# Moving one of the seven products of V, and the first half of P, within an attention block's instruction order

## The reference

```
h    = group_norm(x) * w + b                       # 512 x 1024
q, k, v = split(qkv_w @ h + qkv_b)                 # three times 512 x 1024
attn = softmax(q^T k / sqrt(512))                  # 1024 x 1024
o    = attn @ v^T                                  # 1024 x 512
out  = x + out_w @ o^T + out_b
```

## Time and profile before

| | |
|---|---|
| median of 3 runs | 1997.63 us (1994.39 to 1999.02) |
| the profiled execution | 1995.93 us, its span 1994.1 us |
| TensorE matmul busy | 1977.3 us (99% of the span) |
| VectorE busy | 1644.5 us (82%) |
| ScalarE busy | 1121.0 us (56%) |
| GpSimd busy | 448.8 us (23%) |
| TensorE's granted clock | 0.9 or more of full speed in each of the 40 slices |
| chain that ended last | PE 9%, DVE 4%, ACT 2%, DMA 2%, issue 1% of the span |

### The profile page before, as it was taken

One profiled execution on the slowest core, in us unless ns is written; L12 is line 12 of the kernel. 1 busy time (PEld: TensorE's weight loads), 2 busy tenths in 40 slices (PEclk: granted clock), 3 DMA queues, 4 the chain that ended last, 5 costly groups with the idle time before them and its releaser, 6 DMA issues. The chain is left out here.

```text
span 1994.1 us, 26069 instructions
## 1 busy us (share of the span) xinstructions
PE 1977.3 (99%) x9895; PEld 1679.2 (84%) x9895; DVE 1644.5 (82%) x2010; ACT 1121.0 (56%) x1431; POOL 448.8 (23%) x306
## 2 busy tenths in 40 slices
PE   9999999999999999999999999999999999999999
PEld 7888888888888888888888888887888888878788
DVE  8896987969879698796978879697796987969866
ACT  6564645646465564645656467464565646556461
POOL 1122040231412213131230401314022131221311
PEclk9999999999999999999999999999999999999999
DMA  6305143060431504324042330614306043150411
GB/s 176 128 7 138 49 75 118 6 159 28 75 118 22 170 2 75 118 54 139 6 86 101 70 123 6 146 41 75 118 11 165 17 75 118 20 172 2 75 33 54
DMA packets 102637, 157.89 MB, mean 79 GB/s; under 512 B 49377, under 2 KB 51265, under 8 KB 102513
## 3 DMA queue, kind: packets, MB, share of 16 engines
q0 software_dynamic: 31264, 73.15, 17.5%
q1 hardware_dynamic: 71248, 83.08, 12.9%
HBM read 85.57 MB, written 68.26 MB: 77 GB/s over the span
## 5 line engine op out<-in xcount | busy, mean ns | idle before, releaser
L459 PE MATMUL ring<-r_hi 128*128 128x512 f32 (+1 forms) x1724 | 657.3, 381 | 0.6 <-ACT ring L932 0.4
L460 PE MATMUL ring<-r_lo,r_hi 128*128 128x512 f32 (+1 forms) x1724 | 656.4, 381 | 0.0
L461 PE MATMUL ring<-r_hi,r_lo 128*128 128x512 f32 (+1 forms) x1724 | 656.3, 381 | 0.0
L459 PEld LDWEIGHTS ring<-r_hi 128*128 128x128 f32 x1724 | 324.2, 188 | 64.1 <-DVE r_lo L1478 2.1
L461 PEld LDWEIGHTS ring<-r_hi,r_lo 128*128 128x128 f32 x1724 | 324.2, 188 | 62.0
L460 PEld LDWEIGHTS ring<-r_lo,r_hi 128*128 128x128 f32 x1724 | 324.3, 188 | 61.1
L881 ACT ACTIVATE stage<-ring,keybias 128x512 f32<-128x512 f32 x256 | 175.2, 685 | 164.2 <-PE ring L461 161.5
L1171 POOL PARTITION_ALL_REDUCE stage<-stage x32 | 127.2, 3976 | 460.3 <-DVE stage L1531 460.3
L854 ACT ACTIVATE stage<-ring,by_tile 128x512 f32<-128x512 f32 x120 | 82.5, 687 | 245.9 <-PE ring L461 245.9
L1463 DVE TENSOR_TENSOR r_lo<-stage,r_hi 128x1024 fp32r<-128x1024 f32 x128 | 182.1, 1452 | 0.0
L459 PE MATMUL ring<-h_hi,r_hi 128*128 128x512 f32 x444 | 172.8, 389 | 0.1
(11 more groups left out here) (199 smaller groups left out, 3903.0 us busy)
## 6 DMA issues: line engine op xcount, KB each, us to landing
xs<-x_in SPq DMA_DIRECT2D x64, 512.0 KB, 6.2
out<-xs SPq DMA_DIRECT2D x60, 512.0 KB, 5.4
out<-run_max POOLq DMA_DIRECT2D x60, 256.0 KB, 5.7
inv<-inv_row SPq DMA_DIRECT2D x32, 256.0 KB, 4.1
out<-spare POOLq DMA_DIRECT2D x30, 256.0 KB, 6.9
out<-all_max POOLq DMA_DIRECT2D x30, 256.0 KB, 5.1
r_hi<-g_dram POOLq DMA_DIRECT2D x15, 512.0 KB, 6.4
r_lo<-g_dram POOLq DMA_DIRECT2D x15, 512.0 KB, 6.5
```

What stands on the lines that cost most here:

```text
L459: nc.tensor.matmul(ps_out, st_hi, m_hi, start=first, stop=False, skip_group_check=goes_on)
L460: nc.tensor.matmul(ps_out, st_hi, m_lo, start=False, stop=False, skip_group_check=goes_on)
L461: return nc.tensor.matmul(ps_out, st_lo, m_hi, start=False, stop=last, skip_group_check=goes_on)
```

## The change

In TensorE's list S1 goes from fifth to second place: A11, S1, S2, A12, S3, A22, S4. In ScalarE's list the pieces of P's first half are put in pairs of exponential and high part, and all four come ahead of `copy_third`; `copy_second` comes after the second exponential and not after the first. In VectorE's list the four `p_rest` of the first half come ahead of `add_v22`. Nothing is added or taken away; no tile and no bank changes.

```diff
-V_PRODUCTS = [P_A11, P_S2, P_A12, P_S3, P_S1, P_A22, P_S4]
+V_PRODUCTS = [P_A11, P_S1, P_S2, P_A12, P_S3, P_A22, P_S4]
```

```diff
                     exponential(b, 0, 0)
+                    p_part(b, 0, 0)
+                    exponential(b, 0, 1)
                     copy_second(b, 0)
-                    p_part(b, 0, 0)
+                    p_part(b, 0, 1)
                     copy_second(b, 1)
-                    exponential(b, 0, 1)
-                    p_part(b, 0, 1)
+                    exponential(b, 0, 2)
+                    p_part(b, 0, 2)
                     v11_hi(b, 0)
-                    exponential(b, 0, 2)
+                    exponential(b, 0, 3)
                     v11_hi(b, 1)
-                    p_part(b, 0, 2)
+                    p_part(b, 0, 3)
                     copy_third(b, 0)
-                    exponential(b, 0, 3)
                     copy_third(b, 1)
-                    p_part(b, 0, 3)
                     v22_hi(b, 0)
```

```diff
                     p_rest(b, 0, 0)
+                    p_rest(b, 0, 1)
                     v11_rest(b, 0)
-                    p_rest(b, 0, 1)
+                    p_rest(b, 0, 2)
                     v11_rest(b, 1)
+                    p_rest(b, 0, 3)
                     add_v22(b, 0)
-                    p_rest(b, 0, 2)
                     add_v22(b, 1)
                     v22_rest(b, 0)
-                    p_rest(b, 0, 3)
                     v21_rest(b, 0)
```

## The result

The changed kernel takes 2012.28 us (median of 4 runs, 2011.48 to 2018.74); the kernel before, with one more run, 1996.12 us (1994.39 to 1999.02). The ratio is 1.008, 95% interval 1.0061 to 1.01: 16 us slower. Every ratio here is to the kernel before, run again beside the kernel in question; it is not exactly the quotient of the two medians. The way was forecast, the size was too small (2007), and the range of 1999 to 2015 holds the median.

The account below looks back on a forecast made before the run. TensorE's matmuls were taken as the bound, with 18.0 us of late starts; 25.0 us in V plus 2.7 in T make 27.7, so +9.7 on 1997.6 gives 2007.3, said as 2007, range 1999 to 2015.

Parts of the forecast that it names:

- The bound: Matmuls fill 99% of the span; the change acts only on TensorE's late starts, 18.0 us: 12.0 in T, 6.0 around V.
- ScalarE's chain: In V, one more exponential and high part precede `copy_third`, which starts 9.80 us after the first exponential, 2.03 later than before.
- e: Time from V's first matmul to ScalarE's first exponential, taken as unchanged; 78.3 us summed over the first 14 images.
- The same-time rival: ScalarE's extra pair delays `copy_third` only 1 us, not 2.03, giving 1997 us; chance 0.11, shared with a small e.
- A22's stall: In V, A22 waits e - 3.95 for `copy_third`: 23.0 us over 14 images, 0.6 in the last, without tails.
- tails: Lateness of the matmuls just behind a stall, 0.10 us each time, 1.4 us in V over 14 images.
- Other new waits: In V, S1, S2, S3, S4 and v11_hi's new places add no TensorE wait; the late seed's 0.8 us goes.
- VectorE: Leaves V 0.5 us later (0.1 to 1.0), second add_v12 at e + 17.1; T's waits fall from 12.0 to 2.7 us.
- The clock: Rival, chance 0.06: long stalls drop A22 and S4 to 1.2 GHz, 5.8 us per image, 2019 to 2042 us.
- The sum: TensorE's late starts become 25.0 + 2.7 = 27.7 us against 18.0 before: +9.7 us, 2007 us.
- S1's place: In V, S1 between S3 and A22 had given `copy_third` 2.88 us of cover; moved second, S3 stands directly before A22.

Follow-up runs that it names:

- e1_lists_only: The changed kernel with S1 back in fifth place on TensorE, ScalarE's and VectorE's lists as changed: 2006.42 us, ratio 1.0058.
- e5_scale_early: The kernel before with VectorE's four scalings of A's first half and inverse(b, 1) moved ahead of h_combined: 1983.89 us, ratio 0.9939.
- e8_after_scale_early: The changed kernel with the same early-scaling move on VectorE as e5_scale_early: 2009.47 us, ratio 1.0069.
- e3_warm_pause: The changed kernel with 16 unused matmuls between S3 and A22 in images 1, 2, 11 and 12: 2014.09 us, ratio 1.0093.
- e9_s1_scale_early: The kernel before with S1 moved to second place and VectorE's early scaling of e5_scale_early: 1991.29 us, ratio 0.9968.
- e2_s1_only: The kernel before with only S1 moved to second place, ScalarE's and VectorE's lists as before: 2013.79 us, ratio 1.0092.

## Why the prediction was right in its direction and short in its size

- *The bound.* Right. All differences, to within 1 us, are TensorE's lost time in V and between one V and the next.
- *ScalarE's chain.* Right to 0.02 us: `copy_third` at e + 9.80 to 9.82 in eleven images. The same-time rival (1 us in place of 2.03) is out. In V the lists are what costs most: e1_lists_only has the whole loss in V but 5 us.
- *A22's stall, 23.6 us without tails.* Measured 26.1. Of the 2.5 more, 1.25 is image 1. The step said that no DMA is moved and stopped there; but the moved high part itself waits for a DMA, at `s_us2_out`, and the earlier trace rows stop short of the 0.28 us of that wait in the kernel before. 0.75 is the sum of e (79.05 against 78.3), and 0.5 comes from images 7 and 9, where `copy_second` waited for S2, a wait that I had worked out for the last image only.
- *Other new waits.* Right: S1, S2, S3 and S4 never wait, and image 2's late seed costs nothing.
- *VectorE.* Right: its second `add_v12` is at e + 17.1 in nine images (forecast e + 17.1), later where the clock fell or S2 was waited for, and 3.2 us outside V stay where 2.7 were forecast for T. That the pause in V is what takes T's waits away is borne out by e5_scale_early and e8_after_scale_early.
- *The clock.* This is the step that failed. The forecast had it at nothing and as a rival of 0.06, priced at 5.8 us in each of two or more images. The clock did fall, in three images, behind pauses of 3.84, 3.26 and 3.22 us, for 13, 15 and 26 matmuls: 5.2 us beyond the usual tail. The price per image was a third of the rival's, but the term belonged in the sum. The Trainium skill ("TensorE: Matmul & The Clock Gate", section "HAM oscillation — how this bites in real kernels") warns of pauses of the matmuls for this reason, and the trace agrees that they can bring the clock down. The length alone does not decide it: the clock stayed up behind 3.30 us in image 12, and fell behind 1.91 in e3_warm_pause and 2.29 in e9_s1_scale_early.
- *The sum.* Forecast +9.7; with 2.5 at A22 and 5.2 for the clock it would have been +17.4; the spans differ by 17.1 and the medians by 16.2.
- *S1's place.* The prediction gave it no price of its own. Alone it costs 18.7 us by the medians (e2_s1_only), more than the whole change: S2, now third, holds up `copy_second`, so `copy_third` never starts before 14.2 us behind V's first matmul, and VectorE leaves V late even where e is small. Put beside the lists alone, by the table: in V the lists cost 22.8 us, S1 6.2 and both 28.0; outside V the lists take 12.5 off, S1 adds 13.3, and both together give -11.1. In the changed kernel the longer pause hides S1's part outside V.

## What to carry to other kernels

When the bounding engine waits for a copy, list everything that stands in front of that copy on its own engine, and price a reordering by the steps between starts. Then follow the other engines out of the stage: a stall of the bounding engine gives the late ones time to catch up, so taking it away can bring the cost back as a wait one stage later. The cheapest cure here lay outside the stage whose lists were edited: moving the scaling so that a DMA's latency lies beside other work is worth 13 us (0.9939).

## What the runs showed of the hardware

- The granted clock fell to half behind single pauses of 1.9 to 3.9 us between otherwise dense matmuls, and made the matmuls behind them 1.2 to 2.9 us longer each time, in V and in T alike (in T behind 2.12, 2.40, 2.69 and 2.83 us). Of pauses between 1.9 and 2.4 us some brought it down (1.91, 1.99, 2.12, 2.22, 2.29, 2.40) and others did not (1.94, 2.01, 2.09, 2.17, 2.36), nor did one of 3.30. With 0.43 us of idle left it stayed up. What decides in between stays open.
- e, set by when x arrives from memory, kept its sum over 14 images (77 to 81 us in all kernels but the one with the fullest filler, 73), but not its place: a filler tuned to the images of one profile missed them in the next.
